# Twelve rows of maxima written by two ACTIVATEs of two heads each instead of one of four, in a macaron transformer block on one NeuronCore

## The reference, cut to what matters

```python
q = x @ Wq.T + bq
k, v = jnp.split(x @ Wkv.T + bkv, 2, axis=-1)      # 16 heads of 16
dots = jnp.einsum('bhid,bhjd->bhij', q * scale, k)
dots = jnp.where(causal, MASK_VAL, dots)
attn = jax.nn.softmax(dots, axis=-1)               # over 1024 keys
out = jnp.einsum('bhij,bhjd->bhid', attn, v)
```

## Time and profile before

| | us |
|---|---|
| median of 3 runs | 1573.51 (1569.27 to 1577.14) |
| the profiled execution | 1577.63, its span 1575.9 |
| PE busy | 1344.9 (85%) |
| DVE busy | 1127.1 (72%) |
| ACT busy | 977.3 (62%) |
| POOL busy | 413.3 (26%) |
| mean granted TensorE clock | 0.936 of full speed |

### The profile page before, as it was taken

The page is one execution under the profiler, slowest core; times in us unless marked ns, Lnnn a source line. Parts: engine busy times, 40 slices in busy tenths (PEclk is TensorE's granted clock), DMA queues, the critical chain, the costliest instruction groups (busy, mean ns, idle before and its releaser), DMA issues.

```text
span 1575.9 us, 32770 instructions
## 1 busy us (share of the span) xinstructions
PE 1344.9 (85%) x8464; PEld 581.0 (37%) x8464; DVE 1127.1 (72%) x3677; ACT 977.3 (62%) x1729; POOL 413.3 (26%) x536
## 2 busy tenths in 40 slices
PE   3645799999988899989988898989998998999874
PEld 2422233344433443344333343344433443344332
DVE  6723788777876778767877777767886777768642
ACT  5411377766666667756666767757765766666751
POOL 2311223223321232223321232223322232222110
PEclk9866799999998999999999999999999999999985
DMA  7022412222322222312322232202322232221000
GB/s 243 1 46 60 112 35 61 61 61 61 81 59 63 46 59 72 74 33 61 88 59 55 53 82 62 62 26 61 88 61 53 60 80 61 63 53 40 5 1 27
DMA packets 53969, 95.75 MB, mean 61 GB/s; under 512 B 5776, under 2 KB 47376, under 8 KB 47632
## 3 DMA queue, kind: packets, MB, share of 16 engines
q1 hardware_dynamic: 51744, 92.29, 23.5%
q10 hardware_dynamic: 2032, 1.19, 0.3%
HBM read 59.91 MB, written 33.55 MB: 59 GB/s over the span
## 4 chain that ended last, share of the span: by engine, by line
PE 61%; DVE 12%; issue 11%; ACT 9%; DVEq 3%; DMA 2%; POOL 2%; ACTq 0%; SPq 0%; POOLq 0%
PE o_bank L1178 15%; PE s L1159 14%; PE st L1146 12%; PE misc L1104 7%; PE misc L1125 4%; PE misc L1099 3%; ACT q_stack L804 3%; PE misc L510 3%; DVE s L966 3%; ACT probs L817 2%; DVE max_full L970 2%; ACT parts L780 1%; DVE stats L449 1%; DVE xn L458 1%; DMA part_dram<-parts 1%
## 5 line engine op out<-in xcount | busy, mean ns | idle before, releaser
L817 ACT ACTIVATE probs<-st 128x512 f32<-128x512 f32 (+1 forms) x1216 | 632.3, 580 | 248.6 <-PE st L1146 128.5
L966 DVE CUSTOM_DVE_ANT_0 s<-s,causal 128x128 f32<-128x128 f32 (+3 forms) x1024 | 494.8, 504 | 239.3 <-PE s L1159 221.1
L1159 PE MATMUL s<-k_stack,q_stack 96*128 96x512 bf16 (+3 forms) x1536 | 507.6, 341 | 58.2 <-DVE max_diag L966 32.8
L1146 PE MATMUL st<-q_stack,k_stack 108*128 108x512 bf16 (+3 forms) x1536 | 499.8, 338 | 37.9 <-ACT probs L817 19.6
L970 DVE TENSOR_REDUCE max_full<-s 128x1 f32<-128x512 f32 x512 | 350.1, 684 | 32.5 <-PE s L1159 32.1
L1178 PE MATMUL o_bank<-probs,v_aug 128*17 128x512 f32 (+3 forms) x3072 | 332.7, 506 | 16.5 <-ACT parts L780 10.7
L668 POOL TENSOR_SCALAR_AFFINE_SELECT probs<-probs 128x512 f32<-128x512 f32 x256 | 164.6, 645 | 584.7 <-ACT probs L817 584.1
L1159 PEld LDWEIGHTS s<-k_stack,q_stack 96*128 96x128 bf16 x1536 | 150.4, 99 | 446.6 <-DVE max_diag L966 200.7
L1146 PEld LDWEIGHTS st<-q_stack,k_stack 108*128 108x128 bf16 x1536 | 151.2, 99 | 158.9 <-ACT probs L817 67.2
L804 ACT ACTIVATE q_stack<-misc 12x2048 bf16<-12x2048 f32 x64 | 119.7, 1870 | 77.4 <-PE misc L1131 76.7
L680 POOL TENSOR_TENSOR rest<-qk,parts 128x512 f32<-128x512 f32 x64 | 74.1, 1159 | 356.4 <-ACT parts L780 347.0
(11 more groups left out here) (107 smaller groups left out, 931.9 us busy)
## 6 DMA issues: line engine op xcount, KB each, us to landing
part_dram<-parts SPq DMA_DIRECT2D x128, 192.0 KB, 2.8
q_stack<-part_dram SPq DMA_DIRECT2D x32, 384.0 KB
k_stack<-part_dram SPq DMA_DIRECT2D x32, 384.0 KB
x_all<-x SPq DMA_DIRECT2D x16, 512.0 KB, 5.7
q_stack<-part_dram SPq DMA_DIRECT2D x32, 256.0 KB
k_stack<-part_dram SPq DMA_DIRECT2D x32, 256.0 KB
out<-x_all SPq DMA_DIRECT2D x8, 1024.0 KB, 17.1
q_stack<-part_dram SPq DMA_DIRECT2D x32, 128.0 KB
```

The source lines that it names most:

```text
L817: nc.scalar.activation(probs[:, g % 2, h - part:h + 1, 0:width], st_bank[i % 3][:, 0:share * width] .rearrange("p (h c) -> p h c", c=width ...
L966: nc.vector.tensor_tensor_reduce(out=bank, in0=bank, in1=causal[:, CW - width:CW], scale=1.0, scalar=-BIG, op0=ALU.add, op1=ALU.max, accum ...
L1146: score = nc.tensor.matmul(st_bank[i % 3][:, part * width:(part + 1) * width], k_stack[0:KROWS + MROWS, hg, h, jb * P:(jb + 1) * P], q_sta ...
L1159: nc.tensor.matmul(s_bank[u % 3][:, 0:width], q_stack[0:KROWS, hm, h, ib * P:(ib + 1) * P], k_stack[0:KROWS, hm, h, j0:j0 + width], start= ...
```

## The change

The copy of the twelve rows for four heads (12 x 2048 elements) becomes two copies for two heads each (12 x 1024). The first stands where the old one stood, in the event `use mtr` of unit u. The second is an event of its own, `mev`, in the next unit, u + 1, and only it increments `misc_free`. ACT handles the exponential of unit u + 1, where that unit has one, between the two. No other engine has work for `mev`. In the prologue the two stand back to back.

```diff
@@ step_plan
             put(PLACE["mtr"][hg][c], ("use", "mtr", c))
+            put(PLACE["mtr"][hg][c] + 1, ("mev", c))
@@ prologue_plan
             if u == HALF_UNITS[c] + 6:
-                plan.append((3, "use", "mtr", c))
+                plan += [(3, "use", "mtr", c), (3, "mev", c)]
@@ ScalarE, evict
                 elif what == "mtr":
-                    c, hm = a[0], (hg + 1) % NG
-                    rows = slice(KROWS, KROWS + MROWS)
-                    nc.scalar.activation(q_stack[rows, hm, :, c * CW:(c + 1) * CW],
-                                         misc[rows, :].rearrange("p (o c) -> p o c", o=1)
-                                         .to_broadcast([MROWS, HG, CW]), ACT.Copy)\
-                        .then_inc(misc_free, 1)
+                    max_rows_out(hg, a[0], 0)
+
+            def max_rows_out(hg, c, pair):
+
+                rows, hm = slice(KROWS, KROWS + MROWS), (hg + 1) % NG
+                return nc.scalar.activation(q_stack[rows, hm, 2 * pair:2 * pair + 2, c * CW:(c + 1) * CW],
+                                            misc[rows, :].rearrange("p (o c) -> p o c", o=1)
+                                            .to_broadcast([MROWS, 2, CW]), ACT.Copy)
@@ ScalarE, handle
                 elif kind == "use":
                     evict(b, n, hg, *a)
+                elif kind == "mev":
+                    max_rows_out(hg, a[0], 1).then_inc(misc_free, 1)
```

## The result

The changed kernel takes 1590.2 us (median; 1589.4 to 1593.3), the kernel before 1575.3 in the same measurement. The ratio is 1.0105, 95% interval 1.0083 to 1.0127: slower by 15 us on the medians and by 16 to 17 by the ratio. The forecast was 1586.5, range 1575 to 1593. The profiled executions give 1588.5 after and 1575.9 before, 12.6 us apart. Over the 69 runs of before that the experiments brought, its median is 1574.9. The mean granted clock of the four runs after is 0.933, that of the 69 before 0.940.

What follows compares the result with a forecast made beforehand. PE was taken to pace the kernel, the eviction mattering where PE stands still for it. Terms of 5.7 + 3.1 + 2.6 + 0.7 + 0.9 = 13.0 us on 1573.51 gave 1586.5 us, range 1575 to 1593.

Steps and rivals of the forecast that it cites:

- The cost of one half: Half of the eviction on ACT: 1.025 us, 0.02 us kept from both neighbours; with an exponential between, `misc_free` 0.82 us later.
- step 0, unit 41: Halves back to back, no exponential between: transposes of unit 44 wait 0.15 us longer in six batches, 0.9 us.
- The second rival: Halves overlap their neighbours like other ACT instructions, or DVE's slack takes up more: 5.5 us, 1579; chance 0.20.
- Step 2, unit 40: Fill L1112 of `misc` waits for the second half: 0.82 us more in full, seven batches, 5.7 us.
- The third rival: The longer stop in step 2 brings more half-clock stretches: at most 12.8 us on top, 1599; chance 0.10.
- Step 1: Units 40 and 44: second transposes and L1119 wait for `misc`; 0.39 us in eight batches, 3.1 us (2.0 to 4.2).
- Step 2, unit 14: PE's stop moves from one `st` to the next, 0.33 us later; eight places including one in step 3, 2.6 us.
- The first rival: Not slower: the gain at the first stop is kept in step 0 and step 2; -4.0 us, 1569.5; chance 0.12.
- Step 0, unit 34: Wait of 1.12 us for the exponential shrinks to about 0.27, the `xn` wait grows by as much: gain 0, six batches.
- the places of step 3: Unit 42: 0, hidden behind the loop's return; the `st` place: no cost except 0.33 us in the first batch.

Runs made afterwards that it cites:

- the near places: Split with an exponential between only at step 0 unit 41, step 1 units 40 and 44, step 2 unit 40, against the kernel before: 1591.6 us, ratio 1.0118.
- unit 40 alone: Split with an exponential between the halves only at step 2, unit 40, other evictions whole, against the kernel before: 1586.4 us, ratio 1.0074.
- step 0, unit 34 alone, apart or together: Kernel before, split only at step 0 unit 34: with an exponential between the halves 1567.4 us (ratio 0.9949), or halves back to back 1565.3 us (0.9943).

## Why the prediction was right, and where not

**The cost of one half: right.** 1.025 us were estimated, 1.015 measured on average, 1.018 at most. Between a half and an exponential lie 0.01 to 0.03 us and no overlap, as taken over from the whole eviction: `misc_free` came 2.68 us after the first half's start (2.69 forecast). Two halves in a row do overlap, by 0.1 us: 1.93 us together, and the place of step 0, unit 41 costs between 0.05 and 0.2 us where it was taken at 0.15. The second rival falls, since nothing overlaps at an exponential. The Trainium skill's 93 ns of overlap (ScalarE: Activation LUTs, section What ACT_TABLE_LOAD costs) are met between two halves, and by no eviction here beside an exponential.

**Step 2, unit 40: the mechanism right, the price too small.** The stop of 1.84 us came as 1.82, and nothing hid it. Its price at full clock is 0.80 us. But in the profiled run the delay grew to some 1.7 us in four of seven batches and to 3.3 in one, where a half-clock stretch came to lie behind it. The third rival, with 0.10, was at work together with the forecast, at some two fifths of its price (5.4 us, below, of 12.8). The prediction had named a sign for being wrong here: a mean granted clock that moves by more than 0.005. Over the runs it moved by 0.007; in the two profiled runs alone, 0.936 and 0.934, it doesn't show.

**Step 1: right.** 0.39 to 0.40 us before the second transposes; 0.45 us carried on, inside 0.25 to 0.53. In the first and the last batch it was 0.6 and 1.2, which I hadn't looked at apart.

**Step 2, unit 14: right.** The stop moves by one bank, 0.78 becomes 1.11, and 0.31 us are lost. The first rival (the gain at the first stop is kept) falls here: the two `st` are too near each other.

**Step 0, unit 34: wrong step.** "DVE works through its rows of `xn` without waiting for PE there, so `xn` comes when it did" looked at what DVE waits for, and not at how long its instructions take. The last `xn` took 0.87 us where the others of this place took 0.41, which stood in the trace of before: POOL's select, which an exponential behind the eviction releases, ran into it. With this exponential 0.84 us earlier the select was over when the last `xn` began, and `xn` was done 0.38 us sooner, counted from the eviction's start. Worth -0.36 us in six places at full clock and, tried by itself, 8 us on the median. Most of these 8 us are not explained by the 2.2 of the waits: in the profiled run the place is worth more in four of the six batches (PE is 1.6 to 1.8 us earlier by the next eviction, with a half-clock stretch gone) and costs 1.0 us in one, but the mean granted clock over the runs rose by no more than 0.002. This was the gain that the first rival had, by another way.

**The sum.** The terms forecast came to 13.0 us; at full clock they measured 11.4, with -2.2 in place of 0 at step 0 and 0.6 more elsewhere. Between the means of the runs the change costs 16.0 us. The rest goes with the clock: over all runs of all kernels here, compared within each kernel, the time falls by 8.2 us (standard error 0.4) for each 0.01 more of mean granted clock, and the changed kernel has 0.933 where before has 0.940. That is 5.4 us, leaving 10.6 for the waits themselves. The same sum gives 8.5 of the 16.4 us of the near places to the clock, and 7.9 of the 11.8 us of unit 40 alone. It is a correlation, and a coarse one: it leaves 3.9 us for the waits of unit 40, which come to 5.9 at full clock, and 6 to 8 us for step 0, unit 34 alone, apart or together, whose waits come to 2.2 and 2.8. So the total was close partly by luck: two things that were left out, a gain in step 0 and a loss to the clock, have opposite signs.

Shown by an experiment: that the loss needs the exponential between the halves, that it sits where a fill of `misc` waits, that step 0 gains, and that `xn` is what it gains by. Only read off the traces: that the clock falls because PE stood still longer; no run held the stop and changed the clock alone. One run speaks against a simple rule: with the stop before L1112 taken out of the kernel before, the mean granted clock was 0.937, no higher than the 0.940 with it. Open is what the places of step 3 cost by themselves, where the moved collision is one candidate, and why step 0, unit 34 alone is worth 8 to 9 us.

## What to carry to other kernels

Before splitting an instruction that gives a shared buffer free, list who waits for the buffer and who waits for what is behind the instruction: an exponential let in between is worth nothing if the next bank's wait follows 0.5 us later, and an exponential of 0.6 us let in costs 0.8 us where the next fill waits. Look for an instruction that takes twice its usual time next to another engine's: here one such `xn`, six times in 1575 us, was worth 8 to 9 us, and moving one event moved such a collision to other places. And move the fill rather than the eviction: L1112 seven units earlier gave 6 us alone, and 17 us together with the halves back to back, which gave 5 by themselves.

## What the runs showed of the hardware that was not expected

- A DVE `tensor_scalar` of 128x256 took 0.83 to 0.87 us instead of 0.41 when a GpSimd select began 0.05 to 0.09 us behind it, and 0.41 when the select began 0.13 us behind it; then the select took 0.78 instead of 0.65. 0.06 us on a third engine decided between the two.
- A small stop of PE can be paid twice through the clock. With one stop a batch longer by 0.8 us the mean granted clock of the runs was 0.930 instead of 0.940, and the delay grew to 3.3 us in most batches with the clock at 0.50 behind it. It doesn't hold the other way round: with a stop of 1.02 us a batch taken out the clock was 0.937.
- Single runs of one and the same kernel lie between 1570 and 1582 us with granted clocks from 0.946 to 0.931. So a difference of some us that is read from one profiled run each may be the clock's alone.
- A plain copy of 12 rows overlaps the next copy of the same kind by 0.1 us, and an exponential before or behind it by nothing. The other copies out of PSUM (`o_raw`, 128x512) do overlap the exponentials beside them, by 0.1 us.
